# A gated cross-attention and mixture-of-experts block: setup reordered, maxima regrouped, one variance root moved among the sends

## The reference

```
x = x + tanh(g_xattn) * attention(layernorm(x), ctx, ctx)      # causal, 154 keys
x = x + tanh(g_ffn) * moe(layernorm(x))
attention: Q = q Wq', K = ctx Wk', V = ctx Wv'; softmax(QK'/sqrt(8) where key <= query) V Wo'
moe: top 2 of softmax(x Wr); rank within an expert by cumulative count, kept if <= 160
     gelu(x W1[e] + b1[e]) W2[e] + b2[e], weighted by the two normalised probabilities
```

## Time and profile before

| | us |
|---|---|
| median of 3 runs | 141.88 (141.72 to 141.99) |
| profiled execution, its own time | 142.43 |
| its span, first to last instruction | 140.2 |
| PE, DVE, ACT, POOL busy | 122.2, 103.5, 74.1, 83.6 |

### The profile page before, as it was taken

One profiled execution on the slowest core, in us unless ns is written; L12 is line 12 of the kernel. 1 busy time (PEld: TensorE's weight loads), 2 busy tenths in 40 slices (PEclk: granted clock), 3 DMA queues, 4 the chain that ended last, 5 costly groups with the idle time before them and its releaser, 6 DMA issues.

```text
span 140.2 us, 2215 instructions
## 1 busy us (share of the span) xinstructions
PE 122.2 (87%) x698; PEld 85.1 (61%) x703; DVE 103.5 (74%) x262; ACT 74.1 (53%) x135; POOL 83.6 (60%) x125
## 2 busy tenths in 40 slices
PE   5998978999899999896989979969989999989920
PEld 2443844455455656633449647759889999967710
DVE  5599855947584637399569698793699999999290
ACT  4924667166361447335916397671697777811210
POOL 6679779999999140021678658760077877772000
PEclk9999999999999999999999999999999999999996
DMA  3899880003340000000079601113820001101805
GB/s 97 257 217 228 207 274 4 5 0 91 71 140 0 5 0 0 0 0 2 19 222 301 215 22 39 39 53 65 181 66 29 26 31 43 39 30 25 294 0 150
DMA packets 19017, 12.22 MB, mean 87 GB/s; under 512 B 3381, under 2 KB 16999, under 8 KB 19008
## 3 DMA queue, kind: packets, MB, share of 16 engines
q1 hardware_dynamic: 17344, 9.59, 26.7%
q0 software_dynamic: 1088, 1.86, 4.1%
q10 hardware_dynamic: 576, 0.66, 1.3%
HBM read 7.25 MB, written 5.06 MB: 88 GB/s over the span
## 4 chain that ended last, share of the span: by engine, by line
PE 27%; DVE 22%; POOL 17%; issue 15%; DMA 8%; ACT 6%; POOLq 2%; DVEq 0%; SPq 0%
PE turn L870 5%; POOL results L588 5%; DVE top L1319 5%; POOL slots L558 4%; DMA xn_all<-results 3%; PE turn L883 3%; PE av L926 3%; DVE shared L1621 3%; DMA X<-x 3%; POOL shared L479 2%; PE av L934 2%; PE turn L889 2%; DMA results<-p,result_of 2%; PE turn L1105 2%; PE sc L902 2%
## 5 line engine op out<-in xcount | busy, mean ns | idle before, releaser
L1319 DVE TENSOR_REDUCE top<-turn 128x3 fp32r<-128x462 f32 (+2 forms) x44 | 26.2, 606 | 13.6 <-PE turn L870 7.4
L588 POOL DMA_INDIRECT results<-p,result_of x18 | 19.9, 1103 | 13.6 <-DVE p L1604 8.4
L682 ACT ACTIVATE p_all<-sc 128x1024 f32<-128x1024 f32 x16 | 15.5, 1022 | 16.9 <-PE sc L902 16.9
L558 POOL DMA_INDIRECT slots<-rows,slot_of x16 | 18.6, 1164 | 9.3 <-issue 7.3
L870 PE MATMUL turn<-shared,q_all 128*128 128x462 f32 (+2 forms) x44 | 20.3, 468 | 2.3 <-DVE top L1319 0.8
L1196 PE MATMUL sc<-q_all,w_all 128*128 128x320 f32 x96 | 17.4, 320 | 1.1 <-issue 0.7
L756 ACT ACTIVATE late<-sc,B 128x320 f32<-128x320 f32 x32 | 14.9, 522 | 3.0 <-PE sc L1196 3.0
L1196 PEld LDWEIGHTS sc<-q_all,w_all 128*128 128x128 f32 x96 | 14.2, 188 | 2.2 <-issue 1.9
L870 PEld LDWEIGHTS turn<-shared,q_all 128*128 128x128 f32 x44 | 8.3, 189 | 11.2 <-ACT q_pack_all L645 3.8
L1621 DVE TENSOR_TENSOR shared<-late,shared 128x640 fp32r<-128x640 f32 x16 | 13.1, 821 | 0.3
L549 POOL TENSOR_SCALAR_AFFINE_SELECT p_all<-p_all 128x512 f32<-128x512 f32 x7 | 4.5, 644 | 9.5 <-ACT p_all L682 9.5
(11 more groups left out here) (252 smaller groups left out, 280.5 us busy)
## 6 DMA issues: line engine op xcount, KB each, us to landing
W<-w SPq DMA_DIRECT2D x8, 256.0 KB, 3.2
p_all<-w SPq DMA_DIRECT2D x8, 256.0 KB, 4.4
slots<-slot SPq DMA_DIRECT2D x1, 1386.0 KB, 10.6
results<-zeros SPq DMA_DIRECT2D x2, 512.0 KB, 9.3
parts_all<-slots SPq DMA_DIRECT2D x5, 198.0 KB, 3.0
X<-x SPq DMA_DIRECT2D x2, 256.0 KB, 3.6
xn_all<-results SPq DMA_DIRECT2D x2, 256.0 KB, 4.1
xn_all<-results ACTq DMA_DIRECT2D x2, 256.0 KB, 4.3
```

The costliest lines, as they stand in the source:

```text
L558: nc.gpsimd.indirect_dma_start(out=slots, out_offset=bass.IndirectOffsetOnAxis(ap=slot_of[:, c:c + 1], axis=0), in_=rows[:, t, :], in_offs ...
L588: nc.gpsimd.indirect_dma_start(out=results, out_offset=bass.IndirectOffsetOnAxis(ap=result_of[0:m, e, n:n + 1], axis=0), in_=y[0:m, e % 2, ...
L682: act.activation(p0[:, t, heads, :], sc[:, heads, :], ACT.Exp, scale=SCALE).then_inc(sc_free, 1)
L1319: dve.tensor_reduce(top[:, qt, h0:h0 + nh, 3 * HD], ps[:, 0:nh * keys].rearrange("p (h k) -> p h k", h=nh), AX.X, ALU.max).then_inc(turn_f ...
```

## The change

In the setup:

- x comes in three pieces: tiles 0 and 1 by SP, tiles 2 and 3 by ACT ahead of its two other DMAs, tiles 4 to 7 by SP. DVE clears `slot0` instead of POOL.
- POOL does the packing matrix of the keys first, then `identb`, the first root and the rest. The mask of the last keys is 32 wide with `ident4`, the ten memsets of ones go to DVE, `keys_for_max` is done in pieces of 6, 6 and 16 heads.
- ACT writes the keys' high part itself and DVE takes the low one from PSUM: `kT` goes.
- DVE's second statistics stand behind the first keys. A tile is normalised by one `scalar_tensor_tensor`, with the mean as scalar and `rstd` as a tensor that is repeated, and PE waits tile by tile. The second sequence is normalised behind the first maxima; its rows are turned ahead of group 0, and its queries made within it.
- 44 units of maxima become 40: three heads of tiles 1 to 3 at a time, and head 3 of all three tiles in one. In groups 0 and 1 the packing no longer waits for all maxima of its heads: that of head 7 (tiles 1 to 3), and of heads 10 and 11 in tile 3 of the first sequence, is written after it is read, so nothing is subtracted there, which a softmax allows.

In the attention and behind it: `values` stands ahead of `project_first` and `count(0)`; `choose(0)` goes from group 5 to 6, behind the maxima; each selection of the first sequence is made one place earlier; fills are fewer; the second root stands behind seven sends.

```diff
-        shares = (7, 8, 6, 6, 6, 5, 5, 1)
+        shares = (5, 7, 6, 6, 6, 5, 4, 1)
...
+def units_of_maxima(b, i):
+    first = [(b, (0,), 4 * i, 4, P)]
+    if i == 0:
+        return first + [(b, (qt,), 0, 3, C) for qt in range(1, QT)] + [(b, tuple(range(1, QT)), 3, 1, C)]
+    starts = ((), (4, 7), (10,), (13,))[i]
+    return first + [(b, (qt,), h0, 3, C) for h0 in starts for qt in range(1, QT)]
...
 # POOL
-            for t in range(QT):
+            for t in range(QT - 1):
                 send(0, t)
+            send(0, QT - 1, range(TOPK - 1))
             root(blocks[1], 4)
+            send(0, QT - 1, range(TOPK - 1, TOPK))
...
 # ACT
+            act.dma_start(X[:, 2:QT, :], x_d[:, 2:QT, :]).then_inc(x_in[1], 16)
             act.dma_start(WK[:, :], wkT).then_inc(wk_in, 16)
...
-            act.activation(kT[:, :, :], sc1[:, 0:B * CP], ACT.Copy).then_inc(kT_ready, 1)
+            act.activation(kT_part[:, 0], sc1[:, 0:B * CP].rearrange("p (b k) -> p b k", b=B),
+                           ACT.Copy).then_inc(kT_ready, 1)
...
             pack(0)
+            turned_rows(1)
...
+                if g == 0:
+                    high_queries(1)
                 act.wait_ge(sc_full, 3 * g + 3)
...
 # PE
-            fill(sc[:, 3, :], 12)
+            fill(sc[:, 3, :], 3)
             turn_rows(0)
-            fill(sc[:, 3, :], 4)
+            fill(sc[:, 3, :], 3)
...
             pack(0)
-            pe.wait_ge(consts3, 1)
+            pe.wait_ge(v_ready, 5)
+            turn_rows(1)
...
                 if g < NG:
                     last_scores(g)
+                if g == 0:
+                    queries(1)
...
                 maxima(maxima_beside(g, 3))
+                if 1 <= g <= NG:
+                    values(g - 1)
                 if g == FIRST_TURNED:
...
-                if 1 <= g <= NG:
-                    values(g - 1)
...
-            fill(sc[:, 3, :], 4)
+            fill(sc[:, 3, :], 2)
             count(1)
-            fill(sc[:, 0, :], 8)
+            gather_on_chip(2, 0)
+            fill(sc[:, 0, :], 4)
...
 # DVE
+                dve.scalar_tensor_tensor(xn[:, t, :], X[:, t, :], mean_var[:, t, 0:1],
+                                         rstd[:, t:t + 1].to_broadcast([P, D]), ALU.subtract,
+                                         ALU.mult).then_inc(xn_ready, 1)
...
                 maxima(maxima_beside(g, 1))
+                if g == 0:
+                    low_queries(1)
...
-                if g == FIRST_TURNED:
+                if g == FIRST_PLACED:
                     choose(0)
-                if g == FIRST_PLACED:
                     dve.wait_ge(rstd_ready, 3)
                     scale_difference(0)
                     layernorm(blocks[0], x1, rows, rows_ready)
                     place(0)
+                    select_rows(0, 0)
                 if g == NG - 1:
                     last_later_keys()
-                    select_rows(0, 0)
+                    select_rows(0, 1)
                     low_of_rows(0, *blocks[0])
...
-            select_rows(0, 1)
+            select_rows(0, 2)
             choose_last()
...
-            select_rows(0, 2)
             split_hidden(0, (0,))
```

More of the change, by code:

```diff
@@ L255, in build @@
         turn = [psum(f"turn{n}", [P, 512]) for n in range(2)]
-        x_in = [sem(f"x_in{b}") for b in range(B)]
+        x_in = [sem(f"x_in{n}") for n in range(3)]
         ctx_in, ctx_rep, wk_in, wv_in, wq_in, wo_in, small_in = (
@@ L862, in maxima @@
             def maxima(todo):
-                for b, qt, h0, nh, keys in todo:
+                for b, tiles, h0, nh, keys in todo:
                     ps = bank()
@@ L1294, in pass_bank, with statistics @@
                 banks[0] += 1
-            def statistics(tiles, src):
+            def statistics(tiles, src, landing=False):
                 for t in range(*tiles):
+                    if landing and t in (0, 2, QT):
+                        dve.wait_ge(x_in[t // 2], 16)
                     last = dve.bn_stats(stats[:, t, :], src[:, t, :])
@@ L1316, in maxima @@
             def maxima(todo):
[L1317 removed]
+                for b, tiles, h0, nh, keys in todo:
                     ps = bank()
[L1319 to L1320 removed]
+                    n = nh * len(tiles)
+                    to = top[:, tiles[0], h0:h0 + nh, 3 * HD] if nh > 1 else top[:, tiles[0]:tiles[-1] + 1, h0, 3 * HD]
+                    dve.tensor_reduce(to, ps[:, 0:n * keys].rearrange("p (h k) -> p h k", h=n),
                                       AX.X, ALU.max).then_inc(turn_free, 1)
@@ L1508, in _ @@
             pass_bank()
-            low_queries(1)
+            dve.wait_ge(rstd_ready, 2)
+            for t in range(QT, NT):
+                normalised_rows(t)
             def last_later_keys():
```

217 lines of the change are left out of this document (106 added, 111 removed).

## The result

The changed kernel took 154.26 us (median of 4 executions, 153.09 to 155.18), the kernel before 141.80 in the same comparison: ratio 1.084, 95% interval 1.079 to 1.089, so it is **slower by 12.5 us**. The forecast was 141.0 us, its range 139.4 to 142.3.

A forecast was written before the change was run, and what follows sets the result against it. Bound by POOL's constants until 19.6, PE and DVE exchanging banks to 66, then POOL's sends. Setup's 2.95 us gain is used up by 66 us; the root gives 0.93, taken as 0.9: 141.0 us, range 139.4 to 142.3.

The forecast's parts named there:

- the turning of the second sequence's rows, which wait for four tiles on DVE (0.9): Setup's end: with the packing of group 0 (0.55), this puts group 0's first unit at 16.65.
- POOL should no longer be there: At group 0's start: POOL's key product shrinks from 1540 to 924 elements and ten memsets go to DVE.
- the fourth rival: TensorE's clock falls as setup fills go from sixteen to six: 141.9 to 143.9 us, middle 143.0; chance 0.04.
- PE is never without work for more than about 1 us: The prediction's argument against the clock falling, which it gave a chance of 0.04.
- Setup: Up to group 0's first maxima: queries at 8.45, first maxima end at 15.6, first unit at 16.65; gain 2.95 us.
- Group 0 gives half back: DVE's third unit waits for the second sequence's queries behind both exponentials; 1.5 of the 2.95 us left at group 1's scores.
- The second rival: Slower, the wait in group 0 decides: setup gains only 1.2 to 1.8 us; 142.2 to 142.8, middle 142.4; chance 0.12.
- Group 1: Wider units cost 0.85 us and one more 512-wide mask product 0.3; 0.35 of 1.5 is left.
- Group 2: The regrouped units cost 0.15 us more.
- Groups 3 to 5 and the projection: Units changing places: -0.3, +0.5, -0.3, 0.1 left at 58 us; projection 0.5 later behind group 4's value products.
- The first send: After groups 5 and 6: at 67.7 (67.64 before), with `diff` scaling giving 0.4 back; nothing of the attention part arrives.
- The root and the selections: Second root behind seven sends wins 0.93 us; a selection leaving DVE's list after the sends is hidden by the read-back DMA.

The follow-up runs named there:

- Kernel 7: Kernel 1 plus seven fills on PE where it waits 1.54 us in group 0; 142.32 us, ratio 1.002.
- Kernel 6: The changed kernel with 3 and 18 fills ahead of PE's waits for the second sequence's second and third tile; 147.65, 147.91, 150.91 and 150.95 us.
- 8: Kernel 1 with 12 and 4 fills in the setup, as before the change, group 0's gap left open; 146.13 us, ratio 1.029.
- 1: The changed kernel with POOL waiting for DVE's normalisation ahead of its 924-element product, so all later products run behind it; 145.12 us.
- experiment 3: The kernel before, with the new scalar_tensor_tensor normalisation in the old places; 142.06 us, ratio 0.999.
- 9: Kernel 1 with DVE's low part of the second sequence's queries moved behind its last maximum of group 0; 140.83, 140.87, 140.87 and 144.74 us.
- 4: The kernel before with only the second root moved, behind seven sends instead of eight; 140.95 us, ratio 0.992.
- kernel 5: The changed kernel with only POOL's 2464-element product held until DVE has normalised the second sequence; 149.22 us, ratio 1.050.
- 11: Kernel 9 with two fills in its 0.53 us gap and PE's first projection again ahead of group 4's value products; 140.68 us, ratio 0.987.
- 12: Kernel 11 with the first selection moved behind DVE's last masks and the second into the tail; 139.95 us, ratio 0.982.

## Why the prediction was wrong

The loss parts as follows. Kernel 7 (no collision, clock up) is 0.6 us above the kernel before (142.32 and 141.68, within the error). Kernel 6 adds the collision to it, clock still up: 147.8 in the two executions that kept the clock, 5.5 more; its scores of group 0 begin 5.67 after those of kernel 7. The changed kernel adds the clock: 154.3, 6.5 more.

**The step that failed** is "the turning of the second sequence's rows, which wait for four tiles on DVE (0.9)", with the sentence behind it, "POOL should no longer be there". From the end of the first maxima to the first unit of group 0 the prediction had 1.05 us (15.6 to 16.65); the changed kernel takes 7.24 (15.97 to 23.21) and kernel 7, without the collision, 1.20. DVE's second four tiles had stood in the setup beside POOL's short selects, at 10.83 with 1.49 us, 0.38 more than the first four; the change puts them beside POOL's products for the keys, which block them for 6.0 us (7.14 less 1.13). The price, 0.22 a tile, came from rows with other neighbours. And POOL was there: with a shorter list it comes to its product of 2464 elements at 18.28, where before it came to it within group 0, while DVE read maxima from PSUM:

```profile
21.77 4.32 POOL L479 TENSOR_TENSOR shared<-kT_part,head_mask 128x2464 fp32r<-128x2464 f32 x1
```

A row that hints at it was at hand: four elements of `diff` took 0.61 us on DVE, at 64.04, beside an instruction of POOL, and the prediction used that row for a gain of 0.4 (in the changed kernel they take 0.16), but did not ask which other of DVE's rows now stand beside POOL. No case of the prediction held this.

**The clock** was the fourth rival, at 0.04 and for 2 us. Its mechanism was the right one, its trigger was not: not the fills taken out (8), but PE standing for DVE. "PE is never without work for more than about 1 us" rested on the failed step, and was wrong inside group 0 too, where the forecast itself put DVE's stall over 1 us and did not ask what PE does meanwhile.

**The ledger**, checked against kernel 7, start times in us:

| | before | forecast | kernel 7 |
|---|---|---|---|
| queries, first sequence | 10.31 | 8.45 | 9.28 |
| end of the first maxima | 17.93 | 15.6 | 16.06 |
| first maxima of group 0 | 19.60 | 16.65 | 17.26 |
| scores of group 1 | 27.02 | 25.5 | 26.07 |
| scores of group 2 | 32.10 | 31.7 | 32.36 |
| first projection | 58.19 | 58.6 | 60.08 |
| first send | 67.64 | 67.7 | 69.07 |
| time (median) | 141.7 to 141.9 | 141.0 | 142.32 |

- *Setup*: right in kind, 0.6 us too hopeful at group 0. Of this, 0.4 is in the sum itself: 15.6 and the two terms 0.55 and 0.9 make 17.05, not 16.65, and the prediction names no overlap. DVE begins its first tile at 6.47 in the changed kernel (forecast 6.5), but the four take 1.56 us, 0.39 a tile, outside the bounds of 0.20 to 0.37: they stand beside POOL's mask (`6.80 0.79 POOL L467`), while beside no work of POOL four take 1.13 (1). Between the two forms no gap shows (1.14 and 1.11, experiment 3). The queries follow at 9.2.
- *Group 0 gives half back*: right. 2.34 won at its first maxima, 0.95 left at the scores of group 1 (forecast 2.95 and 1.5). The wait at the low part is there with 1.41 us, and 9 shows that it took 1.0 of the 1.4 lost: moved away, 1.97 of the gain reach group 1. (The second rival's 3.7 us from the first unit to DVE's third maximum does not follow from the prediction's own times, 16.65 and 21.1, which are 4.45 apart; kernel 7 has 4.3.)
- *Group 1*: forecast 1.15 lost, measured 1.21.
- *Group 2*: forecast 0.15 lost, measured 0.81. Half a microsecond of it is the same collision once more, on an instruction of eight elements that ends as POOL's product does (it took 0.41 before at 32.35, itself held to the end of a product at 32.73); PE then waits 0.80 for the maximum behind it:

```profile
32.19 1.28 POOL L538 TENSOR_TENSOR w_all<-W,w_all 128x512 fp32r<-128x512 f32 x1
...
32.61 0.88 DVE L1585 TENSOR_TENSOR std<-mean_var,rstd 128x8 f32<-128x8 f32 x1
...
34.36 0.50 PE L874 MATMUL turn<-shared,q_all 128*128 128x512 f32 x1 [0.80 <-DVE top L1328]
```

- *Groups 3 to 5 and the projection*: forecast 0.6 lost, measured 0.8 (1.07 behind at the scores of group 3, 1.89 at the projection).
- *The first send*: the group of 5 and 6 did give back (1.89 to 1.43 behind), by about the 0.4 of `diff`.
- *The root and the selections*: 0.93 forecast, 0.8 measured by itself (4). In kernel 7 it is lost again on the way. From the first to the fourth start the sends take 5.72 us (69.07 to 74.79), 4.61 before (67.64 to 72.25), as two selections of DVE now run into the start of a send there (68.09 and 70.89, 1.49 us each), one before; so the first send of the second sequence still comes 14.14 us behind the first of all (83.21 and 69.07; before 81.78 and 67.64). What is regained comes later. Before, the last selection stood beside one of the second sequence's sends,

```profile
85.62 1.49 DVE L1443 TENSOR_TENSOR third_first<-place_no,slot_f 128x1280 fp32r<-128x1280 f32 x1
85.73 2.22 POOL L558 DMA_INDIRECT slots<-rows,slot_of  x1 [0.30 <-issue]
```

and in kernel 7 it is made at 74.97. The eight sends of the second sequence take 9.34 us from the first start to the last, 10.94 before, and the last starts 0.17 ahead of before (92.55, 92.72); the profiled executions have spans of 140.0 and 140.2. The prediction put the move of the selections at nothing ("hidden by the read-back DMA of 99.74, whose time hangs on the sends") and did not ask whether it changes the sends: here it costs 1.1 us at one end, and the 1.6 at the other, 1.25 of them by that one send, are more than the root brought.

So without collision and clock the forecast would have been 1.3 us too low and its direction open. The second rival (142.4, "the wait in group 0 decides") comes within 0.1 us of kernel 7, but by luck: it had the setup win 1.2 to 1.8 us, where 2.34 were won and groups 2 to 5 and the projection lost more than forecast, and it took from the root what came from the selections. With both, the time lay 12 us outside the range.

## What to carry to other kernels

Before an instruction of DVE is moved, look at what POOL does at the new place, not only at whether its inputs are there: beside three products of POOL the four tiles here took 7.14 us and not 1.13, and a row whose length fits its size badly (0.61 us for four elements) hints that two engines already collide. The other way round, an instruction of DVE can lengthen what POOL does (a selection beside a send, 2.2 us for 1.0). Then ask of each new wait what PE does meanwhile; here 1.5 us without work at one place cost another 2.8 us by the clock in three executions of four, and seven fills in the gap gave them back.

## What the runs showed of the hardware

- The granted clock fell to half after PE had stood 1.54 us at one place with smaller gaps behind it (1); in kernel 5 it fell behind waits of no more than 0.65 us, and in one execution of four in a kernel whose largest gap there is 0.53 (9; its place of falling is not in the profiled execution). With the same instructions it fell in some executions and not in others; in kernel 6 a wait of 1.55 us was outlasted. Once down it stayed there for 10 us (1), 17 us (5) and 24 us (the changed kernel), with PE busy nearly throughout. The Trainium skill, TensorE: Matmul & The Clock Gate (section HAM oscillation), has idle gaps in PE's work bring the clock down; the traces agree in that. For one gap, kernels 1 and 7 are the measurement: 1.54 us, open or filled, is all that parts them.
- POOL's indirect DMAs are lengthened by DVE's selections, products of two tensors: mostly 0.97 us, up to 2.24 beside one (11, 12). The kernel before has it too: its third send, at 70.47, lasts 1.48 beside the selection of 69.62. While the queue of sends is on the path, a selection that runs into the start of a send is as well. The Trainium skill, SBUF — State Buffer (section SBUF: two separate sides), tells of DMAs issued by GpSimd that wait for DVE, as their descriptors can't be written, for DVE's two-port modes; here it happens beside a product of two tensors.
- Both forms of the normalisation, one with a second tensor and one with two scalars, collide nearly alike with POOL (7.14 and 6.36 us for four tiles), and cost alike in the kernel before (142.06 and 141.77 us).
